# A hybrid layer on one core: another order list, other banks, the loop's joint elsewhere

## What is computed

```python
x = x + attn_a(layernorm(x), Wq, Wk, Wv, Wo, bo)     # linear attention, 16 heads of 64
x = x + ffn(layernorm(x), rhs)                       # int8 matmul, scales by row and by column
x = x + attn_b(layernorm(x), q_w, k_w, v_w, Wq, Wk, g_w, g_b, decay_logits, out_w, out_b, ln_g, ln_b)
x = x + ffn(layernorm(x), rhs)

# attn_a: q, k = relu(x@Wq)+EPS, relu(x@Wk)+EPS; running sums over the rows of k and of k^T v;
#         y = q @ sum(k^T v) / (q . sum(k)), then @ Wo + bo
# attn_b: q, k turned by rope, cut to 16 ranks a head; g = sigmoid(x@g_w.T + g_b)
#         M = M * decay + (g*k*scale)^T v ; y = q @ M, row by row; out = y @ out_w.T + out_b
#         layernorm(x + out) * ln_g + ln_b
```

## Time and profile before

| | us |
|---|---|
| median of 3 runs (3295.21 to 3301.89) | 3299.62 |
| the profiled execution | 3304.08 |
| its span, first to last instruction | 3302.3 |
| TensorE busy | 3054.3 |
| VectorE busy | 2317.0 |
| GpSimd busy | 1046.3 |
| ScalarE busy | 644.7 |

### The profile page before, as it was taken

The page is one execution under the profiler, slowest core; times in us unless marked ns, Lnnn a source line. Parts: engine busy times, 40 slices in busy tenths (PEclk is TensorE's granted clock), DMA queues, the critical chain, the costliest instruction groups (busy, mean ns, idle before and its releaser), DMA issues.

```text
span 3302.3 us, 127393 instructions
## 1 busy us (share of the span) xinstructions
PE 3054.3 (92%) x54932; PEld 2245.8 (68%) x54932; DVE 2317.0 (70%) x4958; ACT 644.7 (20%) x1165; POOL 1046.3 (32%) x1520
## 2 busy tenths in 40 slices
PE   3899999999999999999999999999999999999996
PEld 2667777676676766776766766767767667767674
DVE  7877777667676676776676776666766667766675
ACT  2212211211211212112112112111111121121121
POOL 2133333233233232333332332332332323323333
PEclk8999999999999999999999999999999999999998
DMA  5222112112112122122111122121121211221211
GB/s 173 66 43 50 42 40 48 42 40 49 37 44 50 37 44 47 38 46 47 37 45 42 43 45 42 39 49 37 44 50 34 46 41 43 45 42 40 49 39 29
DMA packets 384392, 153.91 MB, mean 47 GB/s; under 512 B 352800, under 2 KB 361632, under 8 KB 383904
## 3 DMA queue, kind: packets, MB, share of 16 engines
q1 hardware_dynamic: 383904, 146.05, 20.0%
HBM read 45.32 MB, written 16.78 MB: 19 GB/s over the span
## 4 chain that ended last, share of the span: by engine, by line
PE 90%; issue 5%; DVE 3%; DMA 1%; ACT 0%; POOL 0%; POOLq 0%; SPq 0%; DVEq 0%; ACTq 0%
PE bank L774 21%; PE bank L775 21%; PE bank L776 21%; PE bank L1052 7%; PE bank L915 4%; PE bank L871 3%; PE bank L853 2%; PE bank L732 2%; PE bank L886 2%; PE bank L1007 2%; PE bank L839 2%; PE bank L1024 2%; PE bank L983 2%; PE bank L1039 1%; DMA work<-work 0%
## 5 line engine op out<-in xcount | busy, mean ns | idle before, releaser
L1330 DVE TENSOR_SCALAR work<-bank,column 128x256 f32<-128x256 f32 x512 | 222.4, 475 | 316.6 <-PE bank L776 316.4
L774 PE MATMUL bank<-xaT,wq_hi 128*128 128x128 f16 x2048 | 358.4, 220 | 9.9 <-DMA xaT<-xa_split 5.8
L775 PE MATMUL bank<-xaT,wq_hi 128*128 128x128 f16 x2048 | 358.4, 220 | 0.0
L776 PE MATMUL bank<-xaT,wq_lo 128*128 128x128 f16 x2048 | 358.4, 220 | 0.0
L774 PE MATMUL bank<-xaT,wk_hi 128*128 128x128 f16 x2048 | 356.7, 219 | 0.0
L775 PE MATMUL bank<-xaT,wk_hi 128*128 128x128 f16 x2048 | 356.6, 219 | 0.0
L776 PE MATMUL bank<-xaT,wk_lo 128*128 128x128 f16 x2048 | 356.5, 219 | 0.0
L774 PE MATMUL bank<-xbT,wb 128*128 128x128 f16 x2048 | 346.3, 219 | 0.9 <-DMA xbT<-work 0.9
L775 PE MATMUL bank<-xbT,wb 128*128 128x128 f16 x2048 | 346.3, 219 | 0.0
L776 PE MATMUL bank<-xbT,wb 128*128 128x128 f16 x2048 | 346.3, 219 | 0.0
L683 POOL TENSOR_TENSOR work<-work 128x512 f32<-128x512 f32 x128 | 176.9, 1382 | 399.3 <-DVE work L1448 399.3
(11 more groups left out here) (204 smaller groups left out, 8450.6 us busy)
## 6 DMA issues: line engine op xcount, KB each, us to landing
xin<-in_L_attn_a_x SPq DMA_DIRECT2D x64, 256.0 KB, 2.6
out<-work SPq DMA_DIRECT2D x64, 256.0 KB, 2.6
table<-in_tables SPq DMA_DIRECT2D x64, 192.5 KB, 2.5
work<-in_L_attn_a_Wq SPq DMA_DIRECT2D x1, 2048.0 KB, 9.1
work<-in_L_attn_a_Wk SPq DMA_DIRECT2D x1, 2048.0 KB, 14.2
...
work<-work SPq DMA_TRANSPOSE x128, 2.7
```

Source lines behind the costliest of these rows:

```text
L774: nc.tensor.matmul(o, a[0], b[0], start=first, stop=False)
L775: nc.tensor.matmul(o, a[0], b[1], start=False, stop=False)
L776: return nc.tensor.matmul(o, a[1], b[0], start=False, stop=last)
L1330: last = nc.vector.tensor_scalar(qk[:, n, m, :].rearrange("p m t -> p (m t)"), bank[:, 256 * n:256 * n + 256], 0.0, e_[:, :], ALU.max, ALU ...
```

## The change

The list is another one: other places, lags counted from another point of the circle, other banks, another distribution of the weights' preparation over the first slots (0 to 3, before 0 to 2). Before, TensorE's steps in a slot run vb, mm1, qr, kT, ub, mm0, sb, so1, o1, ys0, ys1, yb, wo0, out, wo1, kb, qb, qk0, qk2, qk1, v1, v0, kt0, qk3, gb, u0, s, kt1, kr, so0, u1, o0. After, they run v0, so0, so1, o0, o1, qk2, qb, kb, gb, wo0, wo1, qk3, qk0, vb, kr, qk1, ub, kT, qr, kt1, mm1, mm0, kt0, ys0, sb, ys1, v1, yb, s, u1, u0, out. The number of slots, of turns and of steps is the same. COUNTS follows the new list (for TensorE 59 entries before, 44 after) and is left out here, as are most of the lines of LATE and BORROWED.

```diff
-ORDER = [("u1_e", 1), ("aT0_h", 1), ("vb", 3), ("mm1", 4), ("vb_e", 3), ("qT0_t", 2), ("aT0_l", 1), ("qr", 3),
-         ("kT", 3), ("mm1_e", 4), ("ub", 3), ("qr_e", 3), ("kT_e", 3), ("mm0", 2), ("ld_x", 0), ("ub_e", 3),
-         ("sb", 3), ("so1", 1), ("o1", 1), ("mm1_a", 4), ("mm0_e", 2), ("sb_e0", 3), ("ub_m", 3), ("ys0", 3),
-         ("sb_e1", 3), ("ys1", 3), ("o1_e", 1), ("aT0_t", 1), ("mm0_a", 2), ("yb", 3), ("nb_st", 2), ("nb_rs", 2),
-         ("wo0", 1), ("y_e", 3), ("aT1_h", 1), ("aT1_l", 1), ("nb_ap", 2), ("out", 3), ("xTb_h", 2), ("xTb_l", 2),
-         ("na_st", 0), ("na_rs", 0), ("ld_t", 2), ("na_ap", 0), ("st_o", 4), ("out_e", 3), ("bias", 1), ("aT1_t", 1),
-         ("wo1", 1), ("xTa_h", 0), ("xTa_l", 0), ("no_st", 3), ("no_ap", 3), ("xTb_t", 2), ("ub_a", 3), ("kb", 2),
-         ("no_rs", 3), ("x2l", 2), ("no_f", 3), ("wo_e", 1), ("nf1_st", 3), ("nf0_st", 1), ("kb_e", 2), ("qb", 2),
-         ("nf1_rs", 3), ("nf1_ap", 3), ("nf0_rs", 1), ("nf0_ap", 1), ("xTa_t", 0), ("qk0", 0), ("qk2", 0),
-         ("qk1", 0), ("qk0_e", 0), ("nf1_q", 3), ("v1", 0), ("kb_a", 2), ("xhb", 2), ("kb_h", 2), ("v0", 0),
-         ("qk1_e", 0), ("kt0", 0), ("kb_l", 2), ("qk3", 0), ("qb_e", 2), ("rnd1", 3), ("nf0_q", 1), ("qT1_t", 3),
-         ("v0_e", 0), ("v1_e", 0), ("kt0_e", 0), ("qk2_e", 0), ("gb", 2), ("u0", 0), ("rnd0", 1), ("qk3_e", 0),
-         ("s", 0), ("gb_e", 2), ("u0_e", 0), ("gb_s", 2), ("s_e", 0), ("qb_a", 2), ("kt1", 0), ("qb_h", 2),
-         ("gb_k", 2), ("qb_l", 2), ("kr", 2), ("kt1_e", 0), ("kr_e", 2), ("so0", 0), ("u1", 0), ("o0", 0),
-         ("o0_e", 0)]
+ORDER = [("x2l", 4), ("u0_e", 2), ("xTa_t", 1), ("xTb_l", 3), ("v0", 1), ("bias", 2), ("u1_e", 2), ("so0", 2),
+         ("so1", 2), ("out_e", 4), ("o0", 2), ("o1", 2), ("qk2", 1), ("no_st", 4), ("o0_e", 2), ("xTb_t", 3),
+         ("aT0_h", 2), ("o1_e", 2), ("qb", 3), ("aT0_l", 2), ("no_rs", 4), ("kb", 3), ("aT1_h", 2), ("no_ap", 4),
+         ("no_f", 4), ("aT1_l", 2), ("qk2_e", 1), ("nf1_st", 4), ("nf1_rs", 4), ("ub_a", 4), ("gb", 3), ("qb_e", 3),
+         ("aT0_t", 2), ("aT1_t", 2), ("qb_a", 3), ("nf1_ap", 4), ("kb_e", 3), ("wo0", 2), ("wo1", 2), ("qk3", 1),
+         ("kb_a", 3), ("v0_e", 1), ("gb_e", 3), ("gb_s", 3), ("nf1_q", 4), ("wo_e", 2), ("nf0_st", 2), ("gb_k", 3),
+         ("kb_h", 3), ("nf0_rs", 2), ("kb_l", 3), ("nf0_ap", 2), ("rnd1", 4), ("qk0", 1), ("vb", 3), ("nf0_q", 2),
+         ("ld_x", 0), ("qb_h", 3), ("kr", 3), ("rnd0", 2), ("qb_l", 3), ("qk0_e", 1), ("kr_e", 3), ("qT1_t", 4),
+         ("qk1", 1), ("vb_e", 3), ("qk3_e", 1), ("ub", 3), ("na_st", 0), ("ub_e", 3), ("kT", 3), ("ub_m", 3),
+         ("na_rs", 0), ("qr", 3), ("qk1_e", 1), ("kt1", 1), ("kT_e", 3), ("qT0_t", 2), ("mm1", 4), ("kt1_e", 1),
+         ("mm0", 2), ("qr_e", 3), ("kt0", 1), ("mm1_e", 4), ("mm1_a", 4), ("mm0_e", 2), ("na_ap", 0), ("ys0", 3),
+         ("mm0_a", 2), ("sb", 3), ("ys1", 3), ("sb_e0", 3), ("v1", 1), ("sb_e1", 3), ("nb_st", 2), ("xTa_h", 0),
+         ("kt0_e", 1), ("yb", 3), ("st_o", 4), ("xTa_l", 0), ("s", 1), ("v1_e", 1), ("nb_rs", 2), ("xhb", 3),
+         ("nb_ap", 2), ("y_e", 3), ("ld_t", 2), ("u1", 1), ("u0", 1), ("s_e", 1), ("xTb_h", 2), ("out", 3)]
...
-BANK = {"v0": 4, "v1": 0, "qk0": 2, "qk1": 1, "qk2": 5, "qk3": 2, "kt0": 3, "s_a": 7, "s_b": 2, "o0a": 1, "o0b": 6,
-        "u0a": 0, "u0b": 6, "kt1": 5, "o1a": 5, "o1b": 3, "u1a": 0, "u1b": 5, "wo": 4, "mm0": 2, "qb": 6, "kb": 3,
-        "vb": 7, "gb": 1, "qr": 6, "kr": 3, "sb0": 1, "sb1": 7, "sb2": 0, "sb3": 6, "y0": 2, "y1": 1, "ub0": 4,
-        "ub1": 5, "out": 2, "mm1": 1}
+BANK = {"v0": 6, "v1": 4, "qk0": 2, "qk1": 0, "qk2": 3, "qk3": 5, "kt0": 6, "s_a": 6, "s_b": 7, "o0a": 1, "o0b": 0,
+        "u0a": 0, "u0b": 4, "kt1": 7, "o1a": 4, "o1b": 5, "u1a": 1, "u1b": 5, "wo": 2, "mm0": 4, "qb": 7, "kb": 5,
+        "vb": 7, "gb": 0, "qr": 2, "kr": 3, "sb0": 0, "sb1": 7, "sb2": 5, "sb3": 1, "y0": 2, "y1": 3, "ub0": 6,
+        "ub1": 4, "out": 2, "mm1": 1}
...
 LATE = {
-    (0, "nb_st"): ("load o",),
-    (0, "aT1_h"): ("load rk",),
-    (0, "aT1_l"): ("load rq",),
-    (0, "qk3"): ("max o", "all o"),
...
-    (2, "u0"): ("load wout",),
+    (0, "aT0_t"): ("load o",),
+    (0, "qb_a"): ("max o", "turn decay"),
+    (0, "nf1_ap"): ("all o",),
...
+    (1, "so0"): ("lo o",),
...
+    (3, "rnd0"): ("load wout",),
 }
```

More of the change, by code:

```diff
@@ new lines @@
+    (0, "nf1_ap"): ("all o",),
+    (0, "nb_rs"): ("scale o",),
+    (0, "ld_t"): ("hi o",),
+    (0, "u0"): ("keep decay",),
+    (1, "so0"): ("lo o",),
+    (1, "qk2"): ("load rq",),
+    (1, "nf1_ap"): ("load rhs",),
+    (1, "na_rs"): ("load bk",),
+    (1, "sb_e0"): ("max rhs",),
+    (1, "ld_t"): ("all rhs",),
+    (1, "s_e"): ("columns of rhs", "rows of rhs"),
+    (2, "v0"): ("scale rhs",),
+    (2, "u1_e"): ("round rhs",),
+    (2, "qk2"): ("load g",),
+    (2, "aT1_h"): ("max bk",),
+    (2, "no_ap"): ("load bq", "all bk"),
@@ new lines @@
+    (2, "nf1_rs"): ("scale bk", "hi bk"),
+    (2, "gb"): ("max bq",),
+    (2, "wo1"): ("lo bk",),
+    (2, "gb_s"): ("all bq",),
+    (2, "kb_h"): ("load rk",),
+    (2, "nf0_rs"): ("max g",),
+    (2, "rnd1"): ("scale bq",),
+    (2, "rnd0"): ("all g",),
+    (2, "na_st"): ("hi bq",),
+    (2, "kT_e"): ("lo bq",),
+    (2, "sb_e0"): ("scale g",),
+    (2, "v1"): ("load bv",),
+    (2, "xTa_l"): ("max rk",),
+    (2, "ld_t"): ("all rk",),
+    (2, "s_e"): ("hi g",),
+    (3, "u1_e"): ("max rq",),
@@ L142 @@
+    (3, "so1"): ("scale rk",),
+    (3, "qk2"): ("max bv",),
+    (3, "qb"): ("all rq", "hi rk"),
+    (3, "no_rs"): ("lo g",),
+    (3, "kb"): ("scale rq",),
+    (3, "qk2_e"): ("all bv",),
+    (3, "nf1_rs"): ("lo rk",),
+    (3, "qb_a"): ("hi rq",),
+    (3, "nf1_ap"): ("scale bv",),
+    (3, "nf1_q"): ("lo rq", "hi bv"),
+    (3, "nf0_rs"): ("lo bv",),
+    (3, "rnd0"): ("load wout",),
 }
 TAKEN = ("q", "k", "v", "o", "rhs", "bk", "bq", "g", "rk", "rq", "bv")
[L146 to L155, removed]
+BORROWED = {"decay": (0, "qb_a", 5),
+            "o": (0, "nf1_ap", 0),
+            "rhs": (1, "ld_t", 3),
+            "rhs rows": (1, "s_e", 2),
+            "bk": (2, "no_ap", 1),
+            "bq": (2, "gb_s", 3),
+            "g": (2, "rnd0", 1),
+            "rk": (2, "ld_t", 3),
+            "rq": (3, "qb", 4),
+            "bv": (3, "qk2_e", 4)}
@@ L170 @@
 COUNTS = {
-    "SP": [(2, -3), (2, -2), (2, -1), (2, 0), (2, 1), (2, 2), (6, -5), (6, -2), (10, -4), (10, -2), (10, 1), (10, 3)],
-    "POOL": [(2, -3), (2, -2), (2, -1), (2, 0), (2, 1), (2, 2), (6, -3), (6, 0), (8, -3), (8, 1), (10, -3), (10, -2),
[8 rows of a table removed]
-    "ACT": [(2, -2), (2, -1), (2, 0), (2, 1), (2, 2), (6, -6), (6, -3), (6, -1), (6, 0), (6, 2), (8, -7), (8, -5),
[3 rows of a table removed]
-    "DVE": [(2, -3), (2, -2), (2, -1), (2, 0), (2, 1), (2, 2), (4, -1), (4, 0), (4, 1), (4, 2), (4, 3), (4, 4),
[5 rows of a table removed]
+    "SP": [(2, -3), (2, -2), (2, -1), (2, 0), (2, 1), (8, -4), (8, 0), (10, -14), (10, -9), (10, -5), (10, -4),
+           (10, 0)],
+    "POOL": [(2, -3), (2, -2), (2, -1), (2, 0), (2, 1), (2, 2), (6, -7), (6, -4), (6, -1), (8, -5), (8, -4), (8, -1),
[6 rows of a table added]
+    "ACT": [(2, -3), (2, -2), (2, -1), (2, 0), (2, 1), (2, 2), (6, -4), (6, -1), (6, 2), (8, -6), (8, -5), (8, -3),
+           (8, -2), (8, -1), (8, 1), (10, -11), (10, -9), (10, -8), (10, -7), (10, -6), (10, -4), (10, -3), (10, -2),
+           (10, -1), (10, 2), (32, 0), (32, 16)],
+    "DVE": [(2, -3), (2, -2), (2, -1), (2, 0), (2, 1), (2, 2), (4, -3), (4, -2), (4, -1), (4, 0), (6, -5), (6, -3),
[4 rows of a table added]
 }
```

## The result

The changed kernel takes 3144.7 us (median of 4 runs, 3139.3 to 3145.7) against 3299.4 for the kernel before, run beside it: 0.9529 of the time, 95% interval 0.9512 to 0.9545. That is 155 us less, twice the 75 of the forecast, and outside its range. The profiled execution spans 3142.8 us at a mean granted clock of 0.991 (before 0.970).

What follows compares the result with a forecast made beforehand. It took TensorE's own stream plus its holes to bound the kernel. Terms 24 + 6 + 13 + 8 + 13 - 9 + 18 + 2 = 75 us gave 3225 us against the median 3299.6, range 3185 to 3275.

Steps and rivals of the forecast that it cites:

- the joint: Where the loop jumps back, moved from behind o0 to behind out: queued work covers 0.5 us a turn, 13 us gained.
- the clock behind it: After the jump back, TensorE's fall to half clock stays, a little less of it: 0.3 us a turn, 8 us gained.
- issue stalls in small groups: Within runs of small matmuls, shorter runs cut stalls from about 2 to 1.5 us a turn: 13 us gained.
- the orders (so and o; ys, sb, v1, yb), in the loop: Reordered attention reads and ys, sb, v1, yb steps avoid drains: 24 and 6 us gained over 64 chunks.
- parts outside the loop: Later first product -9 us, weight preparation spread over slots 0 to 3 +18, tail +2.
- Rival C: At the jump back, the queue holds all of out: hole vanishes, 75 us, clock stays up, 44 more; 3106 us, chance 0.05.
- Rival A: The last small-matmul run, yb, s, u1, u0, stalls some 1.4 us in both copies: 3263 us, chance 0.19.
- The first term: Attention reads as so0, so1, o0, o1: each o finds its so a group behind, 0.38 us a chunk, 24 us gained.
- the second: ys0, sb, ys1, then v1, then yb: a drain goes and yb's waits hide, net 0.1 us a chunk, 6 us gained.
- New waits: Waits of yb, so0, so1, wo0 and v0 in the loop: each covered by TensorE work, cost nothing.
- Rivals B and E: A new VectorE wait in each chunk, 3321 us, chance 0.06; and no difference, within 7 us of 3300, chance 0.03.
- First slots and tail: Before and behind the loop: TensorE starts at 46 us, -9 us; weight preparation spread wider, +18; tail +2.

Runs made afterwards that it cites:

- the reversal of two drains: Kernel after, loop's first instruction at place 20 of its 256-instruction block, with so0, o0, so1, o1 for so0, so1, o0, o1: 3091.5 us against 3043.9.
- place 20: Kernel after, only TensorE's loop body placed so that its first instruction has place 20 in its block of 256: 3043.9 us.
- the two reversals: Kernel after with its joint in front of out: 3208.0 us; the same with the loop body at place 20: 3103.3 us.

## Why the prediction was wrong, and where it was right

In us, forecast against measured; the loop's parts are differences of the table, the joint and the clock times 26, the others times 27:

| term | forecast | measured |
|---|---|---|
| the joint | 13 | 3.40 x 26 = 88 |
| the clock behind it | 8 | 1.95 x 26 = 51 |
| issue stalls in small groups | 13 | -2.44 x 27 = -66 |
| the orders (so and o; ys, sb, v1, yb), in the loop | 30 x 54 / 64 = 25 | 2.2 x 27 = 59 |
| parts outside the loop | -9 + 18 + 2 + 5 of the orders = 16 | 27 |
| sum | 75 | 159 |

*The joint.* This step failed. The two bounds, 11 and 89, were right, and the choice near the low end was not. Its reason was that the holes inside small groups "come although wide matmuls stand a few us ahead, which a long queue would have bridged". Those holes are not evidence on the queue: they stand at block borders, and the queue had run dry because a whole block, 128 small matmuls, passes in some 2.2 us (0.017 each) and the next one had not come. Counted as places in the instruction stream, and not as time behind wide work, the holes of the earlier trace rows and their like would have shown it in the trace of before. Rival C had the mechanism and the price of the joint and the clock (75 and 44 us for 88 and 51), at 0.05; its total of 3106 was missed by 39, above all by the stalls, which it left as the forecast had them.

*The clock.* It failed with the joint. With no hole there is no fall: 2.21 us a turn became 0.26. The row taken for it, holds for a hole of 3.15, as `out` at half clock behind an open jump showed once more.

*The stalls.* The sign was wrong, and by more than the lower bound of -25. Rival A named the right run: yb, s, u1 and u0 have a hole of 1.1 us in either copy. It left out so0, so1, o0, o1, another 128 small matmuls in a row, where 1.9 us were lost behind the joint. How many stalls a list has isn't a property of the list: "the rest" in the table stays within 0.5 us over six placings and joints of the new list, while its borders go from 0.04 to 4.4.

*The orders.* The first term was right (24 forecast, 24 to 29 measured, as half of the reversal of two drains), the second too small (6 against 7 to 22). The rest of a turn fell by 2.2 us, 1.1 a chunk, and these two make 0.5 to 0.8 of it. What the other 0.3 to 0.6 is was not tried.

*New waits.* None, as forecast: TensorE is idle for 3.6 us in five turns at place 20, so VectorE, ScalarE and the transposes are never late by more. Rivals B and E fall.

*First slots and tail.* TensorE's first product was expected at 46 us and comes at 50.6:

```profile
50.37 0.45 PE L736 MATMUL bank<-ident,maxima 128*128 128x128 f32 x1 [16.99 <-DVE maxima L1176]
50.61 0.63 PE L771 MATMUL bank<-wv_hi,xaT 128*128 128x512 f16 x1
```

The piece "all o" of slot 0 (L736) stands ahead of v0 on TensorE and waits for VectorE's maxima; the forecast had looked at the weights of v alone. It also had TensorE stand for 45 of the 174 us between 37.2 and the start of slot 4 in before; by the trace TensorE is busy for 142.4 of them, at a mean granted clock of 0.90, and stands for 32. The parts outside the loop gave 27 us for an expected 16, and which of them did was not taken apart.

In all, the forecast made errors of +75, +43 and -79 us on one mechanism, the supply of instructions, and of +34 and +11 on the rest: 84 in the span, 80 in the median. The gain divides like this: neither kernel chose its place. The old one's costs 144 us against the best one tried (3299 and 3155), the new one's 101 (3145 and 3044). So 44 of the 155 us came with the places, and 111 are the new list's, each at its best place tried. Of these some 60 are the joint behind `out`, net of the borders that move with it (59 and 63 in the two reversals).
